# A loop of five passes over pairs of turns, written out as ten turns in the program

## The chip, the cores and the metric

The kernel runs on one core of one Trainium2 chip. A core has five engines that run their own instruction streams and wait for each other by semaphores: PE (TensorE, matrix multiply), DVE (VectorE), ACT (ScalarE), POOL (GpSimd) and SP (SyncE, which here only issues transfers). The metric is the device time of one execution in microseconds (us). Lower is better.

## The reference, cut to what matters

Two transformer-like layers over 32 sequences of 256 tokens with 128 channels, all in fp32. Layer 0 is a linear attention with 32 heads, followed by a gated FFN whose inputs and weights are rounded to four-bit values in blocks of 16. Layer 1 is an RWKV block (a time-mix with a running recurrence, then a channel-mix), followed by the same kind of FFN.

```python
h = _layernorm(x) * (1 + ca) + sa
x = x + ga * attention(h, ...)          # q, k, v, two decaying states by head, den, num
h = _layernorm(x) * (1 + cb) + sb
x = x + gb * fp4_ffn(h, ...)            # down(silu(gate(h)) * up(h)), all quantized
# layer 1: the same frame around an RWKV block
x = x + ga * rwkv(h, ...)               # wkv recurrence, then relu(fk)^2 @ w_value
x = x + gb * fp4_ffn(h, ...)
```

## The kernel before, in words

The 32 sequences are taken two at a time: 16 pairs of 512 tokens. The work on a pair is cut into four stages, and the stages of four neighbouring pairs overlap. A **turn** `n` does, on each engine, the first stage's beginning for pair `n`, the attention of pair `n-1`, the FFN of layer 0 for pair `n-2`, the RWKV block for pair `n-3` and the FFN of layer 1 for pair `n-4`. There are 20 turns, `n` = 0 to 19. A helper `do` leaves out a step whose pair does not exist, so turns 0 to 3 fill the pipeline and turns 16 to 19 empty it. All stages are at work in turns 4 to 15. Turns 0 to 4 also hold the preparation of the weights (`at_start`), of which the last piece, on ACT and PE, is that of the second FFN and ends in turn 4.

Within a turn the order on each engine is written out by hand in a function `body(n)` of that engine. SP's body is one load of `xa` (L383). Each engine's `body` is handed to `turns` (L341 to L350 of the kernel before), which issues turns 0 to 5 with constant `n`, then a hardware loop (`Fori(3, 8)`) whose body is two turns, `2m` and `2m+1`, then turns 16 to 19 with constant `n`. So each engine passes through the loop five times (turns 6 and 7, 8 and 9, 10 and 11, 12 and 13, 14 and 15). It jumps back four times, behind turns 7, 9, 11 and 13, and behind turn 15 it goes on.

In the loop `n` lives in a register. A semaphore is waited for with `after`, `before` or `freed`, all of which end in `wait_ge` on a count such as `turn * per_turn + nth` (L95, L102). With a constant turn the count is a constant in the waiting instruction. In the loop the count needs register arithmetic first. Columns and rows that depend on the pair (L640: a column of the modulation table; L383 and the store of `xb`) are addressed through registers there.

One helper matters besides: `freed_at_ends` waits only if the turn is a Python integer. So PE carries these waits (for PSUM banks) in the constant turns, and leaves them out in the loop, where the other waits already imply them.

Names that the prediction uses: L712 on ACT, `c2`, writes `xs` from a PSUM bank and is the first instruction of ACT's turn (so its starts mark the turns from turn 3 on). L532 on ACT on tile `zn` is the last instruction of ACT's turn. L1542 on DVE, on tile `rope`, is the first of DVE's turn. L1250 on PE multiplies `xs` and waits for L712. On PE the turn's end (L1012, L1016, then the loop's branch) comes some microseconds later.

Of the kernel before, what the change touches and what calls it, by code (L numbers as in the profile page):

```python
# [28 lines left out]
PAIRS = NB // SEQ  # L29
# [107 lines left out]
def build(nc, a, scratch, out):  # L137
    ctx = ExitStack()
    with ctx:
# [201 lines left out]

        def turns(eng, body):

            for n in range(6):
                body(n)
            with eng.Fori(3, PAIRS // 2) as m:
                body(2 * m)
                body(2 * m + 1)
            for n in range(PAIRS, PAIRS + 4):
                body(n)  # L350


# [1 line left out]
        def _(sp):  # L354
# [30 lines left out]
            def body(n):  # L385
                do(load_x, n)
            turns(sp, body)
            for p in range(2):
                sp.wait_ge(s_out[p], 8 * PAIRS)
# [3 lines left out]
        def _(pool):  # L393
# [59 lines left out]
            def body(n):  # L453
# [5 lines left out]
                do(power_a1, n - 2)  # L459
                do(power_a0, n)  # L460
            turns(pool, body)


        @block.scalar
        def _(act):
# [394 lines left out]
            def store(j):  # L860
                act.wait_ge(s_x4, j + 1)
                dst = out_v[j, :, :, :] if isinstance(j, int) else out_v[bass.ds(j, 1), :, :, :].squeeze(0)
                act.dma_start(dst, of_pair(xb, j)).then_inc(s_out[j % 2], 16)
            s.preload_act_table_set("silu_and_others")
            turns(act, body)


# [1023 lines left out]
```

## Time and profile before

| | us |
|---|---|
| median of 3 runs | 1418.07 |
| lowest and highest of them | 1416.13, 1418.85 |
| the profiled execution | 1419.27 |
| its span, first to last instruction | 1417.1 |
| PE busy | 1199.9 (85%) |
| DVE busy | 1123.0 (79%) |
| ACT busy | 1062.4 (75%) |
| POOL busy | 219.3 (15%) |
| mean granted TensorE clock | 0.928 of 2.4 GHz |

The profiled execution is 1.2 us above the median of the three others, and 2.2 us of its time lie outside the span. Busy shares leave out register, branch and semaphore instructions. Those take time on an engine's sequencer and show up, if at all, as idle time "issue": the engine waited for nothing else that the profile knows.

### The profile page before, as it was taken

To read this page: it belongs to the slowest core of one execution; us is meant where nothing else is said; L and a number is where in the kernel's file an instruction comes from. 1 tells how busy PE (TensorE), PEld (TensorE's weight loads), DVE (VectorE), ACT (ScalarE), POOL (GpSimd) and SP (SyncE) were. 2 spreads that over 40 slices of the span, in tenths; PEclk is the share of its full clock that TensorE was granted. 3 is DMA by queue.
4 is the path that set the end of the run, shared out by engine and by line. 5 is a ranking of instruction groups with operands and counts; after the bars stand their busy time and mean duration, and the time that the engine had idled before them with its cause. 6 is when DMAs were issued, how large, how long until landed. Compare 5 with 4: busy or idle time off the path is not lost.

```text
span 1417.1 us, 19485 instructions
## 1 busy us (share of the span) xinstructions
PE 1199.9 (85%) x5610; PEld 723.4 (51%) x5610; DVE 1123.0 (79%) x1619; ACT 1062.4 (75%) x2849; POOL 219.3 (15%) x286
## 2 busy tenths in 40 slices
PE   5465888989899998989898988999898989978664
PEld 2133364655555564646455554646465555546443
DVE  5838587979889797979798897979698898964523
ACT  5252868789797978797897979797888979687553
POOL 1000203021211212030212111020212121110000
PEclk9576998999999999999999999999899999999686
DMA  4000000000000000000000000000000000000000
GB/s 130 0 1 8 1 3 6 2 15 1 15 1 16 1 15 2 8 8 0 16 0 15 0 15 1 15 0 8 9 0 15 0 15 1 8 1 8 1 8 7
DMA packets 21486, 13.45 MB, mean 9 GB/s; under 512 B 1552, under 2 KB 20624, under 8 KB 21392
## 3 DMA queue, kind: packets, MB, share of 16 engines
q1 hardware_dynamic: 12944, 8.29, 1.9%
q10 hardware_dynamic: 8448, 4.20, 1.0%
q14 instruction: 70, 0.57, 0.1%
q8 instruction: 24, 0.39, 0.1%
HBM read 8.28 MB, written 4.19 MB: 9 GB/s over the span
## 4 chain that ended last, share of the span: by engine, by line
PE 63%; ACT 14%; DVE 12%; issue 8%; POOL 2%; SPq 0%; ACTq 0%; DMA 0%; DVEq 0%; POOLq 0%
PE ps L1101 11%; PE ps L1213 6%; PE ps L1310 4%; PE ps L924 4%; PE ps L1303 4%; PE ps L1180 3%; PE ps L1012 3%; PE ps L1016 3%; PE ps L1250 3%; PE ps L904 3%; PE ps L1251 2%; ACT hq L507 2%; PE ps L977 2%; PE ps L938 2%; POOL rstd_of_a L416 2%
## 5 line engine op out<-in xcount | busy, mean ns | idle before, releaser
L1101 PE MATMUL ps<-wguT,hqcol 128*128 128x352 f32 x512 | 175.4, 485 | 20.5 <-ACT hqcol L681 12.5
L1562 DVE TENSOR_TENSOR_SCAN state<-beta,outer 128x512 f32<-128x512 f32 x128 | 149.2, 1206 | 0.0
L1101 PEld LDWEIGHTS ps<-wguT,hqcol 128*128 128x128 f32 x512 | 97.0, 199 | 82.1 <-issue 30.8
L423 POOL TENSOR_TENSOR var_of_f<-squares_f,eps_sum 128x4 f32<-128x4 f32 x32 | 11.9, 373 | 670.2 <-ACT hq L507 670.2
L1412 DVE SCALAR_TENSOR_TENSOR hid<-hidcol,hid 128x1408 f32<-128x1408 f32 (+1 forms) x68 | 106.2, 1566 | 7.7 <-ACT hidcol L698 7.6
L1213 PE MATMUL ps<-hidcol,wdT 128*128 128x256 f32 (+1 forms) x384 | 94.2, 390 | 0.0
L1634 DVE TENSOR_TENSOR hid<-th,ps 128x352 f32<-128x352 f32 x128 | 63.4, 512 | 32.1 <-PE ps L1101 19.6
L904 PE MATMUL ps<-const,hq 128*128 128x128 f32 x128 | 35.2, 347 | 54.2 <-ACT hq L497 53.3
L977 PE MATMUL ps<-state,const 128*32 128x512 f32 x256 | 73.4, 867 | 7.7 <-DVE state L1588 7.4
L1588 DVE TENSOR_TENSOR state<-state,qshare 128x1024 f32<-128x1024 f32 x64 | 76.8, 1222 | 2.2
L705 ACT ACTIVATE hidcol<-ps 128x512 f32<-128x512 f32 x64 | 38.1, 595 | 51.9 <-PE ps L1180 51.9
L689 ACT ACTIVATE th<-ps 128x352 f32<-128x352 f32 x128 | 58.9, 460 | 24.2 <-PE ps L1101 21.4
L1213 PEld LDWEIGHTS ps<-hidcol,wdT 128*128 128x128 f32 (+1 forms) x384 | 71.6, 196 | 8.9 <-ACT hidcol L707 0.2
L640 ACT ACTIVATE gcol<-ps,mod_cols 128x256 f32<-128x256 f32 x64 | 26.8, 470 | 61.7 <-PE ps L1213 61.2
L1412 DVE SCALAR_TENSOR_TENSOR hq<-xmag,hq 128x512 f32<-128x512 f32 x64 | 44.3, 692 | 33.7 <-ACT xmag L693 31.4
L1180 PE MATMUL ps<-const,hid 128*128 128x128 f32 (+1 forms) x384 | 55.3, 283 | 18.3 <-DVE hid L1413 17.1
L924 PE MATMUL ps<-rope,wqk 128*64 128x512 f32 x256 | 64.5, 626 | 1.7 <-DVE rope L1542 1.7
L1180 PEld LDWEIGHTS ps<-const,hid 128*128 128x128 f32 (+1 forms) x384 | 44.8, 141 | 38.7 <-issue 37.3
L1250 PE MATMUL ps<-xs,w_mixed 128*128 128x512 f32 x96 | 54.4, 650 | 10.3 <-ACT xs L712 10.3
L1303 PE MATMUL ps<-xk,fw_key 128*128 128x512 f32 x128 | 62.6, 602 | 0.0
L1310 PE MATMUL ps<-fw_val,ex 128*128 128x128 f32 x512 | 61.4, 278 | 1.3 <-ACT ex L760 1.3
L1310 PEld LDWEIGHTS ps<-fw_val,ex 128*128 128x128 f32 x512 | 58.4, 192 | 7.3 <-issue 5.0
(234 smaller groups left out, 3246.9 us busy)
## 6 DMA issues: line engine op xcount, KB each, us to landing
xa<-in_x SPq DMA_DIRECT2D x16, 256.0 KB, 2.7
out<-xb ACTq DMA_DIRECT2D x16, 256.0 KB, 2.2
const<-in_const SPq DMA_DIRECT2D x1, 848.0 KB, 6.8
state<-in_wmod SPq DMA_DIRECT2D x1, 768.0 KB, 4.6
outer<-in_wqk SPq DMA_DIRECT2D x1, 256.0 KB, 4.7
ex<-in_w_gate_up SPq DMA_DIRECT2D x2, 128.0 KB, 3.0
fw_key<-in_fw_key SPq DMA_DIRECT2D x1, 256.0 KB, 2.9
fw_val<-in_fw_val SPq DMA_DIRECT2D x1, 256.0 KB, 3.7
```

Source lines behind the costliest of these rows:

```text
L904: last = t_.transpose(dst[:, t * P:(t + 1) * P], src[:, t, :], ident)
L924: ins = t_.matmul(dst[f * 64:(f + 1) * 64, :], wqk[:, k, f, :], rope[:, 2 * f + n_, :], start=(n_ == 0), stop=(n_ == 1))
L977: last = t_.matmul(bank("a_n")[c * NH:(c + 1) * NH, :], cst("sel_num"), state[:, m, c, :], start=(m == 0), stop=(m == M - 1), tile_positio ...
L1101: t_.matmul(bank(f"f{l}_{'gu'[g]}{t}")[:, 0:I_FF], hqcol[l][:, t * P:(t + 1) * P], wguT[:, l, g, :], start=True, stop=True).then_inc(s_gu[ ...
L1180: last = t_.transpose(bank(f"f{l}_h{k}{'aac'[c]}")[0:rn, col:col + P], hid[l][:, 2 * k + t, r0:r0 + rn], ident)
L1213: last = t_.matmul(bank(f"f{l}_d")[:, toks], wdT[0:rn, l, c, :], hidcol[l][0:rn, c, toks], start=(c == 0), stop=(c == 2))
L1250: t_.matmul(dst, w_mixed[:, k, 0, :], src[:, :, 1:T + 1], start=True, stop=False)
L1303: t_.matmul(bank(f"c_f{c}"), fw_key[:, c * P:(c + 1) * P], xk[:, :], start=True, stop=True).then_inc(s_fk_mm, 1)
L1310: last = t_.matmul(bank("c_vk")[:, t * P:(t + 1) * P], fkr[:, c, t * P:(t + 1) * P], fw_val[:, c, :], start=(c == 0), stop=(c == F4 // P - 1))
L1412: return v.scalar_tensor_tensor(dst, mag, low, dst, ALU.max, (ALU.add, ALU.subtract)[part])
L1562: return v.tensor_tensor_scan(state[:, m, c, :], beta[:, m, :], src, 0.0, ALU.mult, ALU.add)
L1588: v.tensor_tensor(state[:, m, 2 * h:2 * h + 2, :], state[:, m, 2 * h:2 * h + 2, :], qshare[:, m:m + 1, :].to_broadcast([P, 2, TOK]), ALU.m ...
```

## The change

`turns` now calls `body(n)` with a constant `n` for all 20 turns. Nothing else is edited; the order of work inside `body` is the same.

```diff
         def turns(eng, body):
 
-            for n in range(6):
-                body(n)
-            with eng.Fori(3, PAIRS // 2) as m:
-                body(2 * m)
-                body(2 * m + 1)
-            for n in range(PAIRS, PAIRS + 4):
+            for n in range(PAIRS + 4):
                 body(n)
```

On ACT, at the end of the loop's body and behind it in the program before (`zn` is the tile of the turn's last instruction, `xs` that of the next turn's first):

```order
L538 ACTIVATE norm<-ps,rstd_of_b 128x128 x3
L532 ACTIVATE zn,squares_z<-ps 128x128 [waits normT_z0,z_mm]
L532 ACTIVATE zn,squares_z<-ps 128x128 x3
L346 REGISTER_ALU
L346 COMPARE_AND_BRANCH
L712 ACTIVATE xs<-ps,vec 128x2x256 [waits kvr_mm,normT_b1]
```

The loop's first instructions on ACT, to which that branch jumps:

```order
L346 ISA
L102 ISA [waits normT_b1]
L712 ACTIVATE xs<-ps,vec 128x2x256 [waits kvr_mm]
L95 ISA
L102 REGISTER_ALU [waits betamix_mm]
L102 REGISTER_ALU [waits scan]
L655 ACTIVATE beta<-ps,bbeta 128x2x255 [waits key_scan]
L102 ISA [waits ffn_xqT1]
```

On ACT after the change, between turn 7 and turn 8 (line numbers are five lower):

```order
L533 ACTIVATE norm<-ps,rstd_of_b 128x128 x3
L527 ACTIVATE zn,squares_z<-ps 128x128 [waits normT_z0,z_mm]
L527 ACTIVATE zn,squares_z<-ps 128x128 x3
L707 ACTIVATE xs<-ps,vec 128x2x256 [waits kvr_mm,normT_b1]
L650 ACTIVATE beta<-ps,bbeta 128x2x255 [waits key_scan,scan,betamix_mm]
L676 ACTIVATE hqcol<-ps 128x512 [waits gate_up_mm1,ffn_xqT1]
```

The branch, the jump and the register instructions (`REGISTER_ALU`, `ISA`) are gone; the instructions that compute and what they wait for are the same. DVE and POOL change in the same way.

On PE inside a turn of the loop before (`wy`, `hq` and `wguT` are operands of the RWKV block and of layer 0's FFN):

```order
L95 REGISTER_ALU [waits wkv_y]
L1271 MATMUL ps<-w_oc,wy 128x128 [waits gate_silu1]
L1072 MATMUL ps<-wy,w_o 128x512 [waits ffn_x_scaled0,wkv_y]
L1096 MATMUL ps<-const,hq 128x128 [waits hidden1,ffn_xq0]
L1101 MATMUL ps<-wguT,hqcol 128x352 [waits ffn_xq_copied0,gate_silu1]
```

The same instructions on PE after the change:

```order
L1266 MATMUL ps<-w_oc,wy 128x128 [waits outer,gate_silu1,wkv_y]
L1067 MATMUL ps<-wy,w_o 128x512 [waits hidden1,ffn_x_scaled0,wkv_y]
L1091 MATMUL ps<-const,hq 128x128 [waits outer,hidden1,ffn_xq0]
L1096 MATMUL ps<-wguT,hqcol 128x352 [waits ffn_xq_copied0,wkv_exponents,gate_silu1]
```

Here PE loses the register instructions and gains waits: those of `freed_at_ends` (`outer`, `hidden1`, `wkv_exponents`) now stand in every turn, as they already do in turns 0 to 5 and 16 to 19. No other engine gains a wait.

## Rows read from the trace of the kernel before

**Rows 1.** The page: span, busy time by engine.

```profile
span 1417.1 us, 19485 instructions
PE 1199.9 (85%) x5610; PEld 723.4 (51%) x5610; DVE 1123.0 (79%) x1619; ACT 1062.4 (75%) x2849; POOL 219.3 (15%) x286
```

**Rows 2.** Timeline of ACT, L712 alone: start, duration, idle before and its releaser.

```profile
310.27 0.80 ACT L712 ACTIVATE xs<-ps,vec 128x512 f32<-128x512 f32 x1
...
387.12 0.80 ACT L712 ACTIVATE xs<-ps,vec 128x512 f32<-128x512 f32 x1
...
464.79 0.80 ACT L712 ACTIVATE xs<-ps,vec 128x512 f32<-128x512 f32 x1
...
543.72 0.78 ACT L712 ACTIVATE xs<-ps,vec 128x512 f32<-128x512 f32 x1 [1.63 <-issue]
...
620.98 0.80 ACT L712 ACTIVATE xs<-ps,vec 128x512 f32<-128x512 f32 x1
...
700.06 0.78 ACT L712 ACTIVATE xs<-ps,vec 128x512 f32<-128x512 f32 x1 [1.78 <-issue]
...
777.34 0.80 ACT L712 ACTIVATE xs<-ps,vec 128x512 f32<-128x512 f32 x1
...
1012.74 0.78 ACT L712 ACTIVATE xs<-ps,vec 128x512 f32<-128x512 f32 x1 [1.61 <-issue]
...
1091.65 0.80 ACT L712 ACTIVATE xs<-ps,vec 128x512 f32<-128x512 f32 x1
...
1168.82 0.80 ACT L712 ACTIVATE xs<-ps,vec 128x512 f32<-128x512 f32 x1
...
1246.24 0.80 ACT L712 ACTIVATE xs<-ps,vec 128x512 f32<-128x512 f32 x1
```

**Rows 3.** L712 over the whole run: what its engine sat idle for.

```profile
issue: 6.6, 4
```

**Rows 4.** Timelines of PE and DVE around 700 us, behind turn 9.

```profile
700.89 1.13 PE L1250 MATMUL ps<-xs,w_mixed 128*128 128x512 f32 x2 [2.05 <-ACT xs L712]
...
700.65 1.22 DVE L1542 TENSOR_TENSOR rope<-hcol,const 128x1024 f32<-128x1024 f32 x1 [2.52 <-issue]
```

**Rows 5.** Timeline of PE around 621 us, behind turn 8.

```profile
621.83 1.12 PE L1250 MATMUL ps<-xs,w_mixed 128*128 128x512 f32 x2 [0.16 <-ACT xs L712]
```

**Rows 6.** Chain of waits, 690 to 706 us: start, duration, what.

```profile
697.31 0.97 ACT zn L532 x7
698.28 1.60 issue
```

**Rows 7.** Five stretches: length, busy by engine, PEclk, DMA share, GB/s.

```profile
450.60:457.40 6.80, 6.53 (x22) 2.12 (x23) 6.59 (x17) 5.05 (x14) 4.73 (x5) 0.50 0.01 2
607.60:611.00 3.40, 3.40 (x13) 0.95 (x13) 3.23 (x14) 2.60 (x8) 2.66 (x4) 0.50 0.00 0
996.70:1003.50 6.80, 6.35 (x21) 1.94 (x22) 6.63 (x16) 5.05 (x13) 4.91 (x5) 0.50 0.00 1
1013.80:1017.20 3.40, 3.40 (x6) 1.23 (x6) 0.87 (x1) 2.32 (x7) 0.00 (x0) 0.50 0.01 2
1232.00:1238.90 6.90, 6.51 (x22) 2.10 (x22) 6.87 (x7) 4.07 (x10) 2.80 (x3) 0.52 0.01 1
```

**Rows 8.** Timeline of PE, 1012 to 1018 us.

```profile
1013.57 1.92 PE L1250 MATMUL ps<-xs,w_mixed 128*128 128x512 f32 x2 [1.88 <-ACT xs L712]
```

**Rows 9.** DMA queues of instructions, 310.3 to 387.1 us: packets, MB, share.

```profile
q8 instruction: 3, 0.05, 0.3%
q14 instruction: 2, 0.02, 0.1%
```

**Rows 10.** The same, 621.0 to 777.3 us, where no q8 row stands.

```profile
q14 instruction: 11, 0.09, 0.2%
```

## The prediction

> **What bounds the kernel now.** I read the page first. No engine is busy all the time: PE 85% of 1417.1 us, DVE 79%, ACT 75% [rows 1]. So the length of a turn is set by a chain that goes from engine to engine, and a stall of any one of them in that chain can lengthen it. The next view is the timeline of ACT, for the starts of the turn's first instruction, L712 [rows 2]. Their differences are the lengths of the turns:
>
> - turn 5, constant numbers, all stages at work: 387.12 - 310.27 = 76.85
> - turn 6, the first of the loop: 77.67
> - turn 7, then a jump back: 543.72 - 464.79 = 78.93
> - turn 8, no jump behind it: 77.26
> - turn 9, then a jump: 79.08
> - turn 10, no jump: 77.28
> - turns 11 to 13, with two jumps: 1012.74 - 777.34 = 235.40
> - turn 14, no jump behind it: 78.91
> - turn 15, the loop is left behind it: 77.17
> - turn 16, constant numbers, one stage fewer: 77.42
>
> The ten turns of the loop take 1168.82 - 387.12 = 781.70 us. That is the stretch that the change rewrites. In the timeline the reader is to see that the long turns are those that end in a jump back, and that L712 behind each jump has an idle time (1.61 to 1.78 us where shown) whose releaser is "issue": nothing of another engine was late. Over the whole run "issue" stands before L712 exactly four times, 6.6 us together [rows 3]. There are four jumps back.
>
> Is that idle time on the path? Behind turn 9 PE's L1250 waits 2.05 us for L712, and DVE's L1542 stands idle 2.52 us with "issue" of its own [rows 4]. Behind turn 8, the same place without a jump, PE waits 0.16 us [rows 5]. The chain of waits goes through the last instructions of ACT's turn (L532) and then names 1.60 us of "issue" [rows 6]. So all three engines lose it together, and PE has no work queued to cover it.
>
> **What goes: the jumps.** Take turn 8 (77.26) as a turn of the loop without a jump. Turn 7 is 1.67 longer, turn 9 is 1.82 longer, and turns 11 to 13 are 235.40 - 3 x 77.26 = 3.62 longer for two jumps. Sum 7.1 us. The difference of PE's idle times, 2.05 - 0.16 = 1.89, says the same. When the stall goes, what is late next at that place is the 0.16 us wait of the mid-loop boundary, so I take all of the 7.1. The entry into the loop and its exit (no jump is taken) show no "issue" before L712 at 387.12 and 1168.82 [rows 2], and cost nothing that I can see. SP's and POOL's branches lie in idle time.
>
> The Trainium skill has a price for this too. "Advanced Engine Details and Errata", section Control Flow Timing, gives about 108 ns for a compare-and-branch. By it the five branches would be worth 0.5 us and the time would stay near 1418.7. The trace disagrees by a factor of sixteen per jump.
>
> **What goes: register work.** In the loop the count of most waits, and each address that depends on the pair, is worked out on the waiting engine. Turn 5 has none of it, and also has all of PE's added waits and the same steps as a turn of the loop; it takes 76.85 against 77.26, 0.41 less per turn. For ten turns that is 4.1 us. The bounds: nothing (turn 15, in the loop, is 77.17, and turn 5 is one turn alone) and 4.1. I take 4.1, by the nearest row, and keep 0 for the range.
>
> **What changes of itself: TensorE's clock.** The granted clock falls from 2.4 to 1.2 GHz once in a turn, about 63 us behind L712. In turn 8 it stays there 3.4 us (607.6 to 611.0), in turns 6, 13 and 16 for 6.8 to 6.9 us, and once more for 3.4 us at 1013.8, right behind the fourth jump [rows 7]. What this costs can be read: turn 6 is 0.41 longer than turn 8, turn 16 0.57 longer than turn 5, so about 0.5 us for a long one. The extra one is dearer, because it falls on dense matmuls of 512 columns: L1250's pair takes 1.92 us [rows 8] against 1.13 behind turn 9 [rows 4], and turn 14 is 78.91 - 77.26 = 1.65 longer. That one followed an idle PE behind a jump (1.88 us), so I let it go with the jump: 1.65. The long ones I expect to come more often. With the jumps a pair of turns takes 156.3 us, and the fall comes at nearly the same phase each time; without them each turn is a little over 76.9. I take five long ones in ten turns, 2.5 us. Bounds: none, and ten at 0.57, 5.7 us.
>
> **What is added.** PE gets the waits of `freed_at_ends` in ten more turns. They stand behind other waits of the same instructions, and wait for events that those imply, so none should hold anything; and turn 5, which has them, is the shortest of all. Zero. The program grows by eight turns of code. Whether its fetching costs anything is the first rival.
>
> **The sum.** The ten turns after: 10 x 76.85 + 5 x 0.5 = 771.0, against 781.7. That is 10.7 us less: 7.1 from the jumps, 4.1 from register work, 1.65 from the clock at 1013.8, less the 2.5 of long falls, of which turn 6 had already paid 0.4. From the profiled execution, 1419.27 - 10.7 = 1408.6. That execution is the slowest of the four shown, and may be alone with its fall at 1013.8. From the median without it: 1418.07 - (10.7 - 1.65) = 1409.0. I predict 1409.0. The ends of this case: all turns at 76.85 and no long fall, 1406.1; all at 77.26 and five at 0.57, 775.5 in place of 781.7, 1413.1.
>
> **Rivals.**
>
> *Slower: PE must fetch its straight code.* PE's instructions come by queue q8, the other engines' by q14. In two turns of the loop q8 moves nothing [rows 10]: PE keeps the loop. In the constant turn 5 it moves three packets, at 0.3% of 16 engines over 76.8 us some 1.2 us each [rows 9]. After the change turns 8 to 15 need some 24 such packets more. If PE stood still for each, 29 us would be added, and the time would be 1438. It decides from 10.7 / 24 = 0.45 us lost per packet. Against it: turn 5 had three of them and was shorter than every turn of the loop, so the fetching runs ahead of the work. For the other engines nothing grows: 11 packets of q14 in two turns of the loop against two in turn 5. That the four stalls are fetches of the jump's target fits this, since straight code can be fetched ahead and a jump's target was not.
>
> The Trainium skill has the size of what an engine keeps: "Advanced Engine Details and Errata", section ISA Cache, gives 32 KB in two lines, and 128 KB on TensorE. That speaks against this change on PE, the only engine for which the loop saves the fetching. The absent q8 rows agree with it. It says nothing on whether the fetching shows.
>
> *No change: the stall is hidden anyway.* If a turn were bound by something with slack across its boundary, ACT's and DVE's stalls would be made up later and the time would stay at 1418 to 1419. For it: ACT and DVE are only 75% and 79% busy. Against it: the longer turns are never followed by a shorter one (77.26 and 77.28 behind 78.93 and 79.08).
>
> *Small gain: the jumps alone, and a worse clock.* Turns stay at 77.26 and all ten pay 0.41 for a long fall: 776.7 in place of 781.7, 1414.3. If in addition one fall lands on dense matmuls as at 1013.8, 1415.9, which a measurement would call no change.
>
> *PE's added waits hold it.* If the constant turns were short for another reason and each turn lost even 1 us to them, the gain would be gone: 1419. Turn 16 has them too, and is at 77.42.
>
> **How the numbers follow.** A measurement of this kernel can tell 0.2%, 2.8 us, from no change. My forecast (1406 to 1413) has 0.70. The small gain has 0.13, of which 0.09 still counts as faster and 0.04 as the same. The hidden stall has 0.06, all the same. The fetching has 0.05, slower. The added waits have 0.03, half the same and half slower. A gain of more than 13 us has 0.03. So faster 0.82, same 0.12, slower 0.06. The range from 1404.9 to 1414.6 holds the forecast, most of the small gain and a little of the larger one, and leaves out some 0.2.
>
> **What would show it.** Right: L712 has no "issue" before it anywhere, and its starts are 76.8 to 77.5 us apart from turn 5 to turn 16; DVE's L1542 has no idle time of 2.5 us; PE's wait before L1250 is 0.2 us at every boundary; q8 shows three packets in every turn, and PE has no new idle time beside them; half-clock stretches of 6.8 us stand in about half of the turns. Wrong: turns that are still 77.3 or more without a long fall (no gain from register work); idle time "issue" on PE, ACT or DVE that comes with instruction packets; turns lengthened by more than 0.6 us at a fall of the clock; or four turns of 79 us that stay though the jumps are gone.

## The result, and the profile after

| | before | after |
|---|---|---|
| median, us | 1418.46 (4 runs) | 1404.63 (4 runs) |
| lowest and highest | 1416.13, 1419.54 | 1399.87, 1405.87 |
| profiled execution | 1419.27 | 1405.1 |
| its span | 1417.1 | 1403.2 |

The ratio of the times is 0.9898, with a 95% interval of 0.9872 to 0.9925. The kernel became 13.8 us faster. I had predicted 1409.0 with a range from 1404.9: the direction and the place were right, the size was too small, and the time lies just outside the range. Three terms of the sum, each of 0.9 to 1.7 us, were off in the same direction; the section on the prediction names them.

The starts of L707 on ACT, which was L712 (answers to [rows 2]; columns as there):

```profile
386.55 0.80 ACT L707 ACTIVATE xs<-ps,vec 128x512 f32<-128x512 f32 x1
...
463.40 0.80 ACT L707 ACTIVATE xs<-ps,vec 128x512 f32<-128x512 f32 x1
...
540.25 0.80 ACT L707 ACTIVATE xs<-ps,vec 128x512 f32<-128x512 f32 x1
...
617.10 0.80 ACT L707 ACTIVATE xs<-ps,vec 128x512 f32<-128x512 f32 x1
...
693.95 0.80 ACT L707 ACTIVATE xs<-ps,vec 128x512 f32<-128x512 f32 x1
...
770.82 0.80 ACT L707 ACTIVATE xs<-ps,vec 128x512 f32<-128x512 f32 x1
...
848.27 0.80 ACT L707 ACTIVATE xs<-ps,vec 128x512 f32<-128x512 f32 x1
...
1156.10 0.80 ACT L707 ACTIVATE xs<-ps,vec 128x512 f32<-128x512 f32 x1
```

Turns 6 to 10 take 76.85, 76.85, 76.85, 76.85 and 76.87 us, turn 11 takes 77.45. None has "issue" before it. The boundary behind turn 9 on PE and DVE, where 2.05 and 2.52 us were idle [rows 4]:

```profile
694.80 1.13 PE L1245 MATMUL ps<-xs,w_mixed 128*128 128x512 f32 x2 [0.16 <-ACT xs L707]
...
693.84 1.22 DVE L1537 TENSOR_TENSOR rope<-hcol,const 128x1024 f32<-128x1024 f32 x1
```

PE waits its 0.16 us as it did at a boundary without a jump [rows 5], and DVE does not wait. The queues of instructions in turns 9 and 10, 617.1 to 770.8 us (packets, MB, share), against [rows 10]:

```profile
q8 instruction: 6, 0.10, 0.3%
q14 instruction: 7, 0.06, 0.1%
```

PE now fetches three packets a turn, and the others fetch fewer than the 11 of two turns in the loop. The two kernels in two stretches each, turns 6 to 15 and from turn 16 to the end, the kernel before first (length, busy by engine, granted clock, DMA):

```profile
387.12:1168.82 781.70, 715.43 (x3481) 432.44 (x3480) 682.41 (x951) 643.78 (x1762) 136.07 (x170) 0.97 0.02 7
1168.82:1417.10 248.28, 188.74 (x833) 122.53 (x832) 143.75 (x186) 163.24 (x414) 24.17 (x35) 0.85 0.02 5
```

The changed kernel:

```profile
386.55:1156.10 769.55, 714.88 (x3481) 433.01 (x3480) 680.79 (x951) 644.27 (x1763) 139.84 (x170) 0.97 0.03 8
1156.10:1403.20 247.10, 185.65 (x833) 120.82 (x832) 143.75 (x186) 163.37 (x414) 23.77 (x35) 0.87 0.02 5
```

No engine has less to do. Of the 13.9 us between the spans, 12.15 lie in the ten turns that were a loop. 0.57 lie ahead of them (387.12 against 386.55) and 1.18 behind, in code that did not change.

### The profile page after: what moved, and what is told of

It reads as the page before. It is cut to its first block, busy times and chain, and to the rows that moved or that the text cites. A ratio compares the mean times of both kernels' runs of the same rounds, so it can differ in the third digit from the quotient of the medians.

```text
span 1403.2 us, 18616 instructions
## 1 busy us (share of the span) xinstructions
PE 1193.4 (85%) x5610; PEld 720.9 (51%) x5610; DVE 1121.2 (80%) x1619; ACT 1063.2 (76%) x2849; POOL 222.7 (16%) x286
## 4 chain that ended last, share of the span: by engine, by line
PE 63%; ACT 14%; DVE 12%; issue 7%; POOL 3%; SPq 0%; DMA 0%; ACTq 0%; DVEq 0%; POOLq 0%
PE ps L1096 11%; PE ps L1208 6%; PE ps L919 4%; PE ps L1305 4%; PE ps L1298 4%; PE ps L1175 3%; PE ps L1011 3%; PE ps L1245 3%; PE ps L1007 3%; PE ps L899 3%; PE ps L1246 3%; ACT hq L502 2%; PE ps L933 2%; PE ps L972 2%; POOL rstd_of_a L411 2%
## 5 line engine op out<-in xcount | busy, mean ns | idle before, releaser
L933 PE MATMUL ps<-hcol,wv_rep 128*128 128x512 f32 x128 | 61.4, 602 | 0.0
```

What stands on the lines that cost most here:

```text
L933: ins = t_.matmul(two_banks(("a_v1", "a_v0")[h])[:, n_, :], wv_rep[:, c, :], hcol[0][:, :], start=True, stop=True)
```

## The experiments

The runs of a group share their runs of the kernel before. The medians of these were 1417.82 us (from 1412.21 to 1424.02) for the changed kernel again, the one-pass loops, the loop on ACT alone and PE's waits; 1419.79 for one jump and the other loops on single engines; 1416.11 for the short jumps. Between groups the ratios are the ones to compare. "Written out" below is the changed kernel. Times are medians, ratios are to the kernel before, with a 95% interval. Turns are read from one profile of each.

**The changed kernel again.** No edit.

> The changed kernel as it is, timed beside the others. My theory (jumps 7.1 us, register work 4.1 us, clock): 13 to 15 us below the kernel before, about 1404.5. Rival (part of the first measurement's 13.8 us was luck of the clock's phase): 10 to 12 us below, about 1407.

Measured 1401.83 us (6 runs) against 1417.82: 0.9881 [0.9853, 0.9910]. Turns 6 to 15 took 769.42 us in its profile. That is 16.0 us below, above the 13 to 15 expected; the interval holds the first measurement's ratio too. All its eleven timings, these six with four of the first series and a later profiled execution, lie between 1398.11 and 1405.96.

**Five loops of one pass each.**

```diff
-            for n in range(PAIRS + 4):
+            for n in range(6):
+                body(n)
+            for k in range(3, PAIRS // 2):
+                with eng.Fori(k, k + 1) as m:
+                    body(2 * m)
+                    body(2 * m + 1)
+            for n in range(PAIRS, PAIRS + 4):
                 body(n)
```

> Turns 6 to 15 stand in five hardware loops of one pass each: register work in every turn, but no jump back. My theory: register work costs 0.41 us a turn, so turns are 77.2 to 77.3 us and the time is 4 us above the written-out kernel, near 1408.5; no idle time issue before ACT's first instruction of a turn. Rival (register work costs nothing, the 0.41 was the clock or the single turn compared): turns of 76.85 us, time equal to the written-out kernel within 1 us. Second rival (entering a loop costs as much as a jump back): four stalls of 1.7 us stay and the time is near 1415.

Measured 1404.01 us, 0.9893 [0.9866, 0.9920]. The starts of turns 8 and 9:

```profile
541.49 0.80 ACT L713 ACTIVATE xs<-ps,vec 128x512 f32<-128x512 f32 x1
...
618.34 0.80 ACT L713 ACTIVATE xs<-ps,vec 128x512 f32<-128x512 f32 x1
```

76.85 us. But this experiment doesn't test what it was made for. A loop of one pass has its number worked out when the program is built: on ACT only fifteen register and branch instructions are left in the whole trace, those of the five loops' ends, against a hundred register instructions in each pass of the real loop. So it says nothing on register work. What it does show is that entering a loop and leaving it without a jump back, five times, costs nothing that can be seen.

**One jump: two passes, then written out.**

```diff
             for n in range(6):
                 body(n)
-            with eng.Fori(3, PAIRS // 2) as m:
+            with eng.Fori(3, 5) as m:
                 body(2 * m)
                 body(2 * m + 1)
-            for n in range(PAIRS, PAIRS + 4):
+            for n in range(10, PAIRS + 4):
                 body(n)
```

> The loop on all engines makes two passes (turns 6 to 9, one jump back), turns 10 to 15 are written out. My theory: one jump at 1.8 us and four turns of register work at 0.41 us: 3.4 us above the written-out kernel, about 1408. Rival (the jumps cost nothing of their own and the loss is per turn in a loop, 1.2 us): 4.8 us above. Rival (the gain is an effect of the clock that needs all turns equal): 8 us or more above.

Measured 1409.01 us, 0.9929 [0.9906, 0.9952]. The starts of turns 8, 9 and 10:

```profile
542.50 0.78 ACT L712 ACTIVATE xs<-ps,vec 128x512 f32<-128x512 f32 x1 [1.62 <-issue]
...
619.79 0.80 ACT L712 ACTIVATE xs<-ps,vec 128x512 f32<-128x512 f32 x1
...
697.00 0.80 ACT L712 ACTIVATE xs<-ps,vec 128x512 f32<-128x512 f32 x1
```

Turns 8 and 9, still in the loop, take 77.29 and 77.21. Turn 9 has no jump at either end, and is still 0.36 longer than the 76.85 of a written-out turn. So register work is real. In this profile turns 6 to 15 sum to 773.56 us, 4.0 above the written-out kernel, against 3.4 expected, or 4.8 by the rival of a flat cost per looped turn. The stall that stands at the one jump and nowhere else tells these apart. The times do not: the median lies 7.4 us above the loop on PE alone of the same group (1401.62), more than the 3.4 expected, and the profiled execution (1405.37) was the lowest of six. What the other executions lost beyond the 4.0 us no profile shows.

**The loop on one engine at a time.** In each of these, `turns` keeps the loop of five passes for the engines named (here `act`; then `dve`, `pe`, and `act` with `dve`) and writes out the rest:

```diff
-        def turns(eng, body):
+        def turns(eng, body, eng_name=""):
+            if eng_name in ("act",):
+                for n in range(6):
+                    body(n)
+                with eng.Fori(3, PAIRS // 2) as m:
+                    body(2 * m)
+                    body(2 * m + 1)
+                for n in range(PAIRS, PAIRS + 4):
+                    body(n)
+                return
             for n in range(PAIRS + 4):
                 body(n)
```

On ACT alone:

> The loop of five passes stays on ACT alone; the other engines are written out. My theory: PE waits for ACT's xs, so ACT's stall behind a jump is the one on the path, 1.7 to 1.9 us for each of four jumps, 7.1 us, plus ACT's share of the register work, 0 to 4 us: 7 to 11 us above the written-out kernel, 1412 to 1416. Rival (DVE's longer stall of 2.5 us sets it): less than 2 us above, about 1406.

Measured 1417.48 us, 0.9990 [0.9974, 1.0005]: nearly all of the gain is lost by ACT's loop. The time is above the 1412 to 1416 expected, and 15.7 us above the written-out kernel of the group instead of 7 to 11; the profiled execution took 1414.66 and has its turns 6 to 15 in 780.81 us, 11.4 above the written-out 769.43 (the mean of three profiles, given below). Turns 10, 11 and 12 begin at

```profile
701.46 0.78 ACT L716 ACTIVATE xs<-ps,vec 128x512 f32<-128x512 f32 x1 [1.84 <-issue]
...
778.50 0.80 ACT L716 ACTIVATE xs<-ps,vec 128x512 f32<-128x512 f32 x1
...
857.54 0.78 ACT L716 ACTIVATE xs<-ps,vec 128x512 f32<-128x512 f32 x1 [1.79 <-issue]
```

Turn 10 takes 77.04, turn 11 with its jump 79.04: 2.0 us for ACT's jump. The 0.19 by which turn 10 is over 76.85 is ACT's register work.

On DVE alone:

> The loop of five passes stays on DVE alone. My theory: DVE's stall of 2.5 us before rope is covered in part, because its next instruction waits 1.8 us for PE where there is no jump; some 0.75 us of each jump reaches the turn, 3 us for four, plus DVE's share of the register work (0 to 4 us): 3 to 6 us above the written-out kernel, 1407.5 to 1410.5. Rival (DVE's stall is the one on the path): 7 us or more above, 1412 to 1416.

Measured 1409.52 us, 0.9928 [0.9906, 0.9949]. Turns 9 to 11 of ACT, and DVE's first instruction of turn 10:

```profile
617.29 0.80 ACT L716 ACTIVATE xs<-ps,vec 128x512 f32<-128x512 f32 x1
...
694.34 0.80 ACT L716 ACTIVATE xs<-ps,vec 128x512 f32<-128x512 f32 x1
...
772.09 0.80 ACT L716 ACTIVATE xs<-ps,vec 128x512 f32<-128x512 f32 x1
```

```profile
620.17 1.26 DVE L1665 TENSOR_TENSOR_SCAN epst<-neg_w,ps 128x256 f32<-128x256 f32 x2 [1.76 <-PE ps L1255]
...
696.70 1.22 DVE L1546 TENSOR_TENSOR rope<-hcol,const 128x1024 f32<-128x1024 f32 x1 [2.39 <-issue]
697.85 1.26 DVE L1665 TENSOR_TENSOR_SCAN epst<-neg_w,ps 128x256 f32<-128x256 f32 x2
```

DVE stalls longer than ACT (2.39 us), but turn 10 is only 77.75 against 77.05 for turn 9: 0.7 us per jump reaches the turn. The scan behind `rope` waits 1.76 us for PE where there is no jump (turn 9, the first row) and not at all behind a jump (turn 10), so that wait covers most of the stall. Turns 6 to 15 take 774.73 us, 5.3 above the written-out kernel. Turn 9, into which DVE comes without a jump, is 0.20 over 76.85: DVE's register work.

On PE alone:

> The loop of five passes stays on PE alone, which then fetches no code in it and carries fewer waits but computes their counts. My theory: PE keeps the loop and its jump stalls nothing; register work on PE is ahead of the matmuls, so equal to the written-out kernel within 1.5 us. Rival A (fetching straight code costs PE something): 1.5 to 5 us below the written-out kernel. Rival B (the 0.41 us a turn of register work is PE's): 4 us above it.

Measured 1401.62 us, 0.9872 [0.9851, 0.9894], as the written-out kernel (0.9881). Turns 8, 9 and 10 begin at

```profile
541.97 0.80 ACT L716 ACTIVATE xs<-ps,vec 128x512 f32<-128x512 f32 x1
...
618.80 0.80 ACT L716 ACTIVATE xs<-ps,vec 128x512 f32<-128x512 f32 x1
...
695.59 0.80 ACT L716 ACTIVATE xs<-ps,vec 128x512 f32<-128x512 f32 x1
```

76.83 and 76.79 us: PE's four jumps, its register work and the fetching that it is spared are worth nothing together, within 0.06 us a turn.

On ACT and DVE:

> The loop stays on ACT and DVE, PE, POOL and SP are written out. My theory: all of the loss is ACT's and DVE's, so this is as slow as the kernel before within 2 us: jumps 7.1 and register work 4.1 above the written-out kernel, 1414 to 1418. Rival (PE's register work is a part): 2 to 5 us below the kernel before.

Measured 1421.29 us, 1.0018 [0.9997, 1.0038]. This is the kernel before again, within the 2 us expected of it, though above the 1414 to 1418 that I had named. Turn 10 began at 701.12 and turn 11 at 778.42, 77.30 us, as in the full loop. Its ten turns sum to 784.92 us, more than any profile of the kernel before, with additional stretches at half clock of 3.4 us right behind two of the jumps (544.1 and 1015.2 us). So the loops on PE, POOL and SP have no part in the loss that shows.

**PE's added waits left out in turns 6 to 15.**

```diff
 def freed_at_ends(eng, sem, turn, per_turn=1, nth=None):
 
-    if isinstance(turn, int):
+    if not 6 <= TURN[0] < PAIRS:          # TURN[0] is the turn that is being written
         freed(eng, sem, turn, per_turn, nth)
```

> Everything written out, but PE's extra waits (those of freed_at_ends) stand only in turns 0 to 5 and 16 to 19, as in the kernel before. My theory: they wait for what other waits imply and cost nothing: equal to the written-out kernel within 1 us, turns of 76.85. Rival (each wait takes PE's sequencer some 50 ns and 24 more of them a turn are in part on the path): turns of 76.3 to 76.7 us and 2 to 5 us less.

Measured 1402.42 us, 0.9896 [0.9872, 0.9920]. Turns 7 and 8:

```profile
459.36 0.80 ACT L711 ACTIVATE xs<-ps,vec 128x512 f32<-128x512 f32 x1
...
536.13 0.80 ACT L711 ACTIVATE xs<-ps,vec 128x512 f32<-128x512 f32 x1
...
612.92 0.80 ACT L711 ACTIVATE xs<-ps,vec 128x512 f32<-128x512 f32 x1
```

76.77 and 76.79 us, 0.07 less than 76.85. That is 0.7 us for ten turns, which the times can't resolve. The loop on PE alone, which leaves the same waits out, has turns of nearly the same length (76.79 and 76.83).

**The loop with constant columns.** The kernel before, but in the loop ACT's modulation reads the columns of the first pair, so no address is computed.

```diff
-                cols = slice(k, k + 1) if isinstance(i, int) else bass.ds(k, 1)
+                cols = slice(k, k + 1) if isinstance(i, int) else slice(q, q + 1)
```

> The kernel before, its loop kept, but ACT's modulation (affine) reads the columns of the first pair in every turn of the loop, so that ACT computes no address there and only the counts of its waits; this leaves out the use of the right column. My theory: of the 0.42 us that a turn without a jump is longer in the loop, about half is ACT's, and it is the two address instructions ahead of each L640 activation; turns 8, 10, 12 and 15 come down from 77.27 to about 77.05. Rival (it is the counts of the waits): they stay at 77.2 or more. The jumps cost 1.8 us in either case.

One profiled execution took 1416.95 us, beside 1419.55 of the kernel before. Turns 8 and 12:

```profile
544.26:621.36 77.10, 70.36 (x344) 42.75 (x344) 68.24 (x96) 64.31 (x177) 11.99 (x15) 0.98 0.03 7
857.52:934.62 77.10, 70.19 (x344) 42.77 (x344) 68.25 (x96) 64.40 (x177) 11.98 (x15) 0.98 0.02 7
```

77.10 against 77.27, and turn 15 takes 76.89 against 77.17: ACT's part of the register work is for the most part the address instructions ahead of its modulation, as expected. Turns 10 and 14 (78.74 and 78.04) are of no use here: each has an additional stretch at half clock of 3.4 us right behind a jump.

**Short jumps.** The written-out kernel, with a loop of three passes over one fulfilled wait behind turns 7, 9, 11 and 13 on ACT and DVE.

```diff
             for n in range(PAIRS + 4):
                 body(n)
+                if held is not None and n in (7, 9, 11, 13):
+                    with eng.Fori(0, 3):
+                        eng.wait_ge(held, 1)
```

> The written-out kernel with a small loop put behind turns 7, 9, 11 and 13 on ACT and on DVE: three passes over one wait that is long fulfilled, so two jumps back at each place, to a target a few instructions away. My theory (a jump costs what it does because its target has to be fetched again): the short jumps cost nothing of note, under 0.5 us at each place; turns 7, 9, 11 and 13 stay within 0.5 us of 76.85 and no packets of instructions follow; time within 2 us of the written-out kernel, 1400 to 1406. Rival (any jump back drains or restarts the engine's sequencer for 1.7 us): these turns are 78.5 us or more, over 80 if each of the two jumps pays, and the time is 7 us or more above.

Measured 1403.18 us, 0.9900 [0.9876, 0.9924]. Behind turn 7, DVE and ACT:

```profile
536.94 1.26 DVE L1540 TENSOR_TENSOR rope<-hcol,const 128x1024 f32<-128x1024 f32 x1 [0.24 <-issue]
```

```profile
536.72 0.80 ACT L710 ACTIVATE xs<-ps,vec 128x512 f32<-128x512 f32 x1
```

Two jumps back to a near target leave ACT without a gap and DVE with 0.24 us, where one jump to the far head of the loop cost 1.6 to 1.9 and 2.4 to 2.7. The jump itself is not what costs. It is not quite free either: turns 10, 12 and 14, each behind a place with two short jumps, take 77.16, 77.17 and 77.16 us, 0.3 more than 76.85. Of the turns that I had expected within 0.5 us of 76.85, turn 9 missed by a little: 77.43, with a stretch of 6.8 us at half clock in it.

The sequencers' own instructions show what stands in the stall. In the kernel before, behind turn 9, these are the loop's branch and the first instruction at its target, on three engines (operation, duration in ns, start):

```profile
L346 ACTq COMPARE_BRANCH  x1: 45/45/45, 697.2 to 697.2; - x1
L346 DVEq COMPARE_BRANCH  x1: 63/63/63, 697.5 to 697.5; - x1
L346 ACTq FUSED_REGOPS  x1: 50/50/50, 699.9 to 699.9; - x1
L346 DVEq FUSED_REGOPS  x1: 85/85/85, 700.5 to 700.5; - x1
L346 PEldq COMPARE_BRANCH  x1: 220/220/220, 706.9 to 706.9; - x1
L346 PEldq FUSED_REGOPS  x1: 68/68/68, 707.2 to 707.2; - x1
```

From branch to target ACT issues nothing for 2.7 us and DVE for 3.0, while PE goes on after 0.3, and so do POOL and SP after 0.2 (689.7 to 689.9 and 681.5 to 681.6 us). They all jump back over their whole body of two turns, and PE's body is the longest, so distance alone is not the price. In the gap of ACT and DVE, 697.2 to 700.5 us, and in that of ACT when the loop is on ACT alone, 698.6 to 701.3, stand packets of instructions:

```profile
q14 instruction: 2, 0.02, 2.0%
```

```profile
q14 instruction: 1, 0.01, 0.8%
```

It is so behind every jump on ACT or DVE in all eight profiles that have one: 2.4 to 2.7 us without an instruction on ACT, 2.7 to 3.0 on DVE, and at least one packet of q14 in each gap. There is none in the gaps of 0.1 to 0.2 us behind the short jumps.

**Two more profiles of the kernel before, one of the changed one**, to see how the parts outside turns 6 to 15 move.

> A second profile of the kernel before, read in three parts: up to turn 6, turns 6 to 15, and from turn 16. My theory (what the changed kernel gained outside turns 6 to 15 is chance): turns 6 to 15 take 780 to 783 us again, and the parts before and behind, 387.1 and 248.3 in the first profile, move by 1 us or more. Rival (the change helps these parts too): they stay within 0.3 us of the first profile.

> A third profile of the changed kernel, read in the same three parts. My theory: turns 6 to 15 take 769 to 770.5 us, and the head and the tail fall in the range of the other profiles whatever the kernel (382.6 to 388.4 and 243.8 to 250.0). Rival: head and tail are the shorter ones of that range each time (386.0 or less and 247.1 or less).

> A third profile of the kernel before, to the same end as the second: turns 6 to 15 in 780 to 783 us; head between 382.6 and 388.4, tail between 243.8 and 250.0, neither always longer than in the changed kernel.

| profile | start of turn 6 | turns 6 to 15 | from turn 16 |
|---|---|---|---|
| before | 387.12 | 781.70 | 248.28 |
| before, 2nd | 386.59 | 780.14 | 247.67 |
| before, 3rd | 387.77 | 781.75 | 248.18 |
| after | 386.55 | 769.55 | 247.10 |
| after, 2nd | 387.53 | 769.42 | 246.93 |
| after, 3rd | 387.68 | 769.33 | 246.99 |

Means: 781.20 and 769.43 us in the ten turns, so 11.8 us are the change's own, as good as constant. The head is alike in both. The tail is 1.0 us shorter in the mean after the change, and each of its three is below each of before, so neither side of my expectation held for it: it does not look like free chance, though it is the same code. The spans' means differ by 12.7 us. But over the profiles of all kernels here the head moved from 382.6 to 388.6 and the tail from 243.8 to 250.0. Most of the other written-out profile's low span (PE's waits left out, 1397.7 us) is a head of 382.61.

## Why the prediction was right or wrong

The mechanism held: the jumps and the register work cost what the sum says. What failed is the remainder of the sum, in three terms: 1.65 us left out of the median's gain, 2.5 us set for long stretches at half clock that cost 1.05, and nothing set for the parts outside the ten turns, which gained 0.9 in the mean.

**Bottleneck and place: right.** ACT's stall behind a jump sets the turn, DVE's lies mostly beside it, PE keeps its loop. The kernel with the loop on ACT alone is as slow as the kernel before, and the one with the loop on PE alone is as fast as the written-out one.

**The jumps, 7.1 us: right.** All four stalls are gone. That they are fetches of the target was argued ahead. It is now supported from three sides: packets of q14 in every gap between branch and target on ACT and DVE, short jumps that cost next to nothing and bring no packets, and PE's jumps that cost nothing where q8 moves nothing. Packets of instructions were not slowed or sped up on purpose, and one took some 0.3 to 0.6 us of a gap of 2.4 to 3.0; what fills the remainder is not shown. The engine's own number is 1.8 to 2.0 us a jump for ACT and 0.7 to 0.9 for DVE alone. These do not add: with both loops a jump cost 1.6 to 1.8. The 7.1 had also counted in turn 13's long stretch at half clock, some 0.4 us; in the kernel with one jump turn 7 is 1.66 us longer than turn 8, and four times that is 6.6.

**Register work, 4.1 us: right.** The clean turn went from 77.26 to 76.85, exactly the turn that turn 5 had shown. ACT and DVE have about 0.2 us each, ACT's for the most part by its addresses. PE has none that shows.

**TensorE's clock, 1.65 gained and 2.5 lost: mis-sized.** This is the term that failed in the ten turns. I expected five long stretches at half clock at 0.5 us each. The profile after has three, at 834.4, 988.0 and 1141.6 us, and the other two profiles have two each. The first two of the three:

```profile
834.40:841.20 6.80, 6.80 (x24) 2.37 (x24) 6.69 (x17) 5.13 (x13) 4.32 (x5) 0.50 0.00 0
988.00:994.80 6.80, 6.21 (x20) 1.83 (x20) 6.72 (x16) 5.22 (x14) 4.92 (x5) 0.50 0.00 0
```

Together the ten turns are 769.55 - 768.5 = 1.05 us above ten of 76.85, not 2.5. In the two other profiles it is 0.9 and 0.8. That is 1.45 us of the miss. The turns with a long stretch were 0.1 to 0.6 us longer, so the count and the price were both too high. One of the two rows behind the price misled: turn 16 has a stage fewer than turn 5, and its long stretch cost 1.0 us, not 0.57 (77.42 and 77.33 us with it, 76.42 in the second profile of the kernel before, where the fall lasts 3.4 us).

**Profile against median: wrong.** From the median I took off only 9.05 us, because I held the additional fall at 1013.8 [rows 7] for an accident of the profiled execution. The third profile of the kernel before has the same one, with a turn 14 of 78.96 us; the second has none (77.28). So it belongs to many executions of this kernel, and the gain of the median should have held most of its 1.65 us. This is the largest of the three terms: the full 10.7 us taken from the median would have given 1407.4.

**Outside the ten turns: not in the sum at all.** The first pair of profiles gained 1.75 us there, the three pairs 0.9 in the mean. A part of it can be read in turn 16: 77.42 and 77.33 us in two of the profiles before, with the long stretch at half clock, and 76.08 to 76.47 in all three after, with a short one. That the stretches fall elsewhere because the turns ahead changed their length is argued; no run tested it.

These account for the miss in the profiled pair: 10.7 predicted, 1.45 from the long stretches, 1.75 from outside the ten turns, and 0.3 outside the spans, together the 14.2 us between 1419.27 and 1405.1. Counted from the median, 1409.0 less 1.65, 1.45 and 0.9 is 1405.0, against 1404.63 measured.

Four of the eleven timings of the written-out kernel fall to 1398 to 1400. Their mean granted clocks are 0.936 to 0.940, those of the other seven, with the three profiled ones, 0.929 to 0.932. The kernel before moves with its clock in the same way: in the first group from 1424.02 us at 0.922 to 1412.21 at 0.933. At 0.930 or 0.931 it takes 1416.2 to 1417.8 there and the changed kernel 1404.2 to 1406.0, which is again some 11 to 12 us. So the gain that does not depend on the clock is about 11.8 us, and what a median shows above it goes with a higher mean clock. Why the clock is higher in some executions stays open. One profile at 0.940, of the kernel with PE's waits left out, has a head of 382.61 us and six falls in its ten turns, where the written-out kernel's profiles have nine or ten.

**The rivals.** PE's fetching of straight code costs nothing that shows: turns with three packets are as short as any (76.78 us with PE's waits left out), and sparing them by a loop on PE gains no more than leaving out its waits does. The price of the Trainium skill's "Advanced Engine Details and Errata", section Control Flow Timing, 108 ns for a compare-and-branch, is not contradicted by the short jumps (two jumps back idled ACT for nothing and DVE for 0.24 us). The page does not say for which jumps it holds; for the kernel's own jumps on ACT and DVE it does not. The section ISA Cache of the same page of the Trainium skill fits the difference: TensorE, for which it states 128 KB, jumped for nothing, and ACT and DVE, for which it states 32 KB, did not.

## What to carry to other kernels

If a loop's body is long and a turn's end is tight, look for idle time "issue" (here 1.6 to 2.7 us) in front of the first instruction of each pass, count the jumps, and ask of each engine whether another waits there. The engine that is waited for comes first, but it is not all: with ACT written out and the loop left on DVE, the ten turns had 6.5 of the 11.8 us, with ACT and DVE written out all of them. A loop whose body the engine keeps (PE here) can stay. When a forecast says that a disturbance of the profiled run is an accident, bound the sum by the case that it is not.

## What the runs showed of the hardware that was not expected

- Two short jumps back on ACT fitted entirely beside its running activations; one long jump back idled it 1.6 to 1.9 us and DVE 2.4 to 2.7 us.
- With 18 more separate wait instructions per turn on PE (1249 against 1069 in the whole trace) a turn was 0.07 us longer; if they are the cause, that is an estimate of 4 ns each, though one takes 51 ns on PE's sequencer.
- The part from turn 16 on took 243.8 to 250.0 us over fifteen profiles with the same code there. It went with the share of it at half clock: 243.8 and 244.2 us at a granted clock of 0.89, 246.8 to 247.7 at 0.86 or 0.87, 248.1 to 250.0 at 0.85.
